# The end of a middle layer and the sums of the next similarity, written as one program for each engine

## The reference, cut to what matters

```
x: 64 batches of 128 x 512 (f32)
layer 0:  A = top-k graph of the mean similarity of x's columns;  x = layernorm(x + An-mixing(x) * adj + bias)
layer 1:  per batch: K = mix of two row-normalised 128x128 kernels of x;  x = layernorm(x + K x W_V' W_O')
layer 2:  as layer 0, on the x that layer 1 gives (a new similarity, a new graph)
layer 3:  x = layernorm(x + (adj*adj)' x + bias)
similarity: x_norm = x / norm over the batches;  S = sum over batches and rows of x_norm x_norm'  (512 x 512)
```

## Time and profile before

| | us |
|---|---|
| median of 3 runs (lowest to highest) | 1667.31 (1666.35 to 1667.31) |
| the profiled execution, own time | 1667.62 |
| its span in the trace | 1665.8 |
| busy in the span: PE | 1513.1 (91%) |
| DVE | 1224.0 (73%) |
| ACT | 926.9 (56%) |
| POOL | 549.3 (33%) |

### The profile page before, as it was taken

How to read it: one execution, slowest core, us unless ns; L and a number is a source line. 1 busy time by engine, 2 the same in 40 slices (tenths; PEclk the granted TensorE clock), 3 DMA queues, 4 the chain that set the end, 5 groups by cost and what they waited for, 6 DMA issues and landing times. The chain is left out here.

```text
span 1665.8 us, 27716 instructions
## 1 busy us (share of the span) xinstructions
PE 1513.1 (91%) x7736; PEld 1255.1 (75%) x7736; DVE 1224.0 (73%) x3081; ACT 926.9 (56%) x1651; POOL 549.3 (33%) x749
## 2 busy tenths in 40 slices
PE   6899999589999999999999999993999971999996
PEld 4677787478888888888888888872888871777774
DVE  5788799647666667666667666653676997799997
ACT  7775455225556554556554556553333870577775
POOL 6553001011223322223322223321000000899997
PEclk9999999689999999999999999996999895999998
DMA  6220393311121221121221121101541000344442
GB/s 216 102 89 1 144 404 147 99 54 44 51 70 63 76 76 42 51 72 63 76 76 40 51 73 63 39 27 63 196 141 38 0 0 6 128 145 145 139 149 103
DMA packets 80630, 148.23 MB, mean 89 GB/s; under 512 B 8448, under 2 KB 8576, under 8 KB 80576
## 3 DMA queue, kind: packets, MB, share of 16 engines
q1 hardware_dynamic: 80576, 147.56, 25.5%
HBM read 97.06 MB, written 50.46 MB: 89 GB/s over the span
## 5 line engine op out<-in xcount | busy, mean ns | idle before, releaser
L814 POOL TENSOR_TENSOR rs_a<-ve_a,neghalf 128x1 f32<-128x1 f32 x64 | 35.1, 548 | 408.8 <-DVE nm_a L808 408.8
L226 PE MATMUL bank<-xn_lo,xn_hi 128*128 128x512 f32 (+1 forms) x640 | 145.4, 358 | 5.4 <-DVE xn_lo L203 5.2
L198 ACT ACTIVATE xn_hi<-xn 128x512 fp32r<-128x512 f32 x128 | 80.6, 630 | 116.7 <-DVE xn L191 116.5
L1176 ACT ACTIVATE xo<-xo,nb_b,rs_b 128x512 f32<-128x512 f32 x64 | 52.2, 816 | 144.9 <-POOL nb_b L816 144.9
L1692 POOL TENSOR_TENSOR xw_lo<-xres,xw_hi 128x512 fp32r<-128x512 f32 x64 | 83.0, 1297 | 131.4 <-ACT xw_hi L1657 131.4
L226 PEld LDWEIGHTS bank<-xn_lo,xn_hi 128*128 128x128 f32 x640 | 102.8, 193 | 19.5 <-DVE xn_lo L203 10.4
L1631 PE MATMUL l_ps<-an_hi,xw_hi 128*128 128x512 f32 x256 | 105.2, 411 | 10.1 <-POOL xw_lo L1692 8.7
L960 PE MATMUL l_ps<-an_hi,xw_hi 128*128 128x512 f32 x256 | 103.5, 404 | 11.8 <-DVE xw_lo L1327 11.5
L217 PEld LDWEIGHTS bank<-xn_hi 128*128 128x128 f32 x512 | 95.2, 191 | 24.1 <-ACT xn_hi L198 7.5
L536 DVE MATCH_REPLACE8 work<-best,work 128x520 f32<-128x520 f32 x160 | 108.2, 684 | 0.0
L322 POOL TENSOR_TENSOR sq_lo<-sq,sq_hi 128x512 fp32r<-128x512 f32 x64 | 87.3, 1380 | 61.3 <-ACT sq_hi L289 61.1
(11 more groups left out here) (238 smaller groups left out, 4743.9 us busy)
## 6 DMA issues: line engine op xcount, KB each, us to landing
xr<-in_x SPq DMA_DIRECT2D x32, 512.0 KB, 3.4
xw_dram<-stage SPq DMA_DIRECT2D x64, 256.0 KB, 6.0
stage<-xw_dram SPq DMA_DIRECT2D x64, 256.0 KB, 2.8
stage<-in_x SPq DMA_DIRECT2D x64, 256.0 KB, 2.7
between<-xo SPq DMA_DIRECT2D x64, 256.0 KB, 2.0
xres<-between SPq DMA_DIRECT2D x32, 512.0 KB, 3.7
xin<-between SPq DMA_DIRECT2D x64, 256.0 KB, 2.7
out<-xo SPq DMA_DIRECT2D x64, 256.0 KB, 2.0
```

Source lines behind the costliest of these rows:

```text
L198: self.nc.scalar.activation(self.hi[:, i % 4, :], self.xn[:, i % 4, :], ACT.Copy).then_inc(self.hi_ready, 1)
L226: mm = self.nc.tensor.matmul(out, h[:, c * P:(c + 1) * P], l[:, a:b], start=(i == 0 and c != 1), stop=False, skip_group_check=True)
L814: nc.gpsimd.tensor_tensor(root, var_eps, neghalf, ALU.pow).then_inc(root_ok, 1)
L1176: nc.scalar.activation(xo[:, i, :], xo[:, i, :], ACT.Identity, scale=rs_b[:, i:i + 1], bias=nb_b[:, i:i + 1]).then_inc(xo_ok, 1)
```

## The change

The function `second_similarity` is gone; its work is done inside `gnn_layer_pair`, without a barrier before it. To make room, the big tiles get fixed places on one ground of 80 slots of 512 values: `xres` takes slots 0 to 63, and the weights and tiles of layers 0 and 1 lie in the same slots. Each pair of batches is brought back once the tile under it has been used for the last time. The PSUM banks are shared too: the sums use banks 0 to 6, which are tiles of the middle layers before.

The turn (14, 15, none) is called `nearly`. In it the norms of the first 56 batches are brought in, rooted, capped, inverted and split, and batch 0 is spread, normalised and given its high part. The turn (15, none, none) is called `last`. In it each engine walks through the 64 batches of the sums, and the table `TAIL` says behind which batch each piece of the last group's chain C stands. The norms of the last 8 batches come when the last group's sums of squares are stored, and are prepared in batches 38 to 51. In `last`, `l1` and the last `squares` use bank 7 alone, so that `l1(i)` waits for `residual_b(i-1)`.

No barrier is left ahead of the sums; the one between the sums and the second `adjacency` stays. Elsewhere only the places of tiles and the numbers of PSUM banks differ, and `diagonals` writes its products into `a_l` and `a_g` and not into a tile of its own. Six semaphores that were cleared at the end of the middle layers are now cleared at the end of the kernel.

The core of the diff:

```diff
+AN, U, WOV, AFTER_WEIGHTS = 0, 8, 18, 26
+AFTER_RING = AFTER_WEIGHTS + RING
+STAGE, PARTS, NORMED, SLOTS = 64, 72, 76, 80
+TAIL = {"scaled": 0, "k_sum": 1, "k_turned": 1, "kt": 3, "l1": [3, 7, 11, 15], "residual": [5, 9, 13, 17],
+        "stats": [6, 10, 14, 18], "norm": [8, 12, 16, 20], "square": [9, 13, 17, 21], "squares": 25, "sums_out": 27,
+        "root": 38, "cap": 39, "invert": [40, 43, 46, 49], "rows_hi": 50, "rows_lo": 51}
...
@@ SyncE, behind the loop of full turns @@
+            turn(groups - 3, None, groups - 1)
+            sp.wait_ge(l0_made, 2 + nb)
+            for p in range(4):
+                bring_back(p)
+            sp.wait_ge(filled[0], 1)
+            sp.wait_ge(n2_stored, 16 * (1 + groups - 2))
+            norms(0)
+            for i in range(GRP):
+                sp.wait_ge(xo_ok, GRP * (groups - 2) + i + 1)
+                store(GRP * (groups - 2) + i, i)
+            sp.wait_ge(y_made, 2 * CH * groups)
+            for p in range(4, 8):
+                bring_back(p)
+            store_sums(groups - 2)
+            for p in range(8, nb // 2):
+                sp.wait_ge(sums.normed, 2 * (p - 8) + 2)
...
+                if p in (13, 15, 17, 19):
+                    i = (p - 13) // 2
+                    sp.wait_ge(xo_ok, GRP * (groups - 1) + i + 1)
+                    store(nb - GRP + i, i)
+                if p == 22:
+                    store_sums(groups - 1)
+                if p == 24:
+                    sp.wait_ge(filled[1], 1)
+                    sp.wait_ge(n2_stored, 16 * (1 + groups))
+                    norms(1)
+                if p == known // 2:
+                    for i in range(GRP):
+                        sp.wait_ge(stored[i], 16 * (groups + 1))
+                bring_back(p)
@@ TensorE, in turn @@
+                if last:
+                    spread(1)
+                    for i in range(nb):
+                        if i == 0:
+                            pe.wait_ge(kl_ok, nb)
+                        sums.squares(pe, i)
+                        if i + 2 < nb:
+                            spread(i + 2)
+                        if i == 0:
+                            pe.wait_ge(v_lo_ok, GRP + nb)
+                            pe.wait_ge(n2_out, groups)
+                        sums.crosses(pe, i)
+                        if i == TAIL["k_turned"]:
+                            k_turned()
+                        if i in TAIL["l1"]:
+                            l1(TAIL["l1"].index(i))
+                        if i == TAIL["squares"]:
+                            squares(0)
+                            squares(1)
+                    return
...
                     m_g_turned()
                     a_s_turned()
+                    if nearly:
+                        spread(0)
                     vprod(3)
@@ ScalarE, in turn @@
+                def n_root(k):
+                    act.wait_ge(n2_in[k], 32)
+                    nc.scalar.activation(nrm[k][:], nrm[k][:], ACT.Sqrt).then_inc(n_rooted[k], 1)
...
                 if B:
                     y_hi(1)
+                if nearly:
+                    n_root(0)
+                    nc.scalar.activation(warm[:], s.inv_s2[:], ACT.Exp)
...
                     y_hi(3)
+                if nearly:
+                    rows_hi(0)
                 if C:
                     for i in range(GRP):
                         square(i)
...
                     exp_g()
+                if nearly:
+                    sums.high_part(act, 0)
@@ VectorE, in turn @@
+                if last:
+                    for i in range(nb):
+                        if i:
+                            dve.wait_ge(x_back[i // 2 % 8], 16 * (i // 16 + 1))
+                            sums.normalise(dve, i, xres[:, i, :])
+                            sums.low_part(dve, i - 1)
+                        if i == 0:
+                            coefficients()
+                        if i == TAIL["k_sum"]:
+                            kernel_sum()
+                        if i == TAIL["kt"]:
+                            kt_lo()
+                        if i in TAIL["residual"]:
+                            residual_b(TAIL["residual"].index(i))
+                        if i in TAIL["stats"]:
+                            stats_b(TAIL["stats"].index(i))
...
...
                     stats_b(0)
                     stats_b(1)
+                if nearly:
+                    n_cap(0)
                 if B:
                     y_lo(2)
+                if nearly:
+                    n_invert(0, 0)
+                    n_invert(0, 1)
...
                     stats_b(2)
                     stats_b(3)
+                if nearly:
+                    n_invert(0, 2)
+                    n_invert(0, 3)
...
                     y_lo(3)
+                if nearly:
+                    rows_lo(0)
...
                     kernel_l()
+                if nearly:
+                    dve.wait_ge(x_back[0], 16)
+                    sums.normalise(dve, 0, xres[:, 0, :])
+                if B:
                     kernel_g()
```

More of the change, by code:

```diff
@@ L65, in scope, with ground, place @@
     return sb, ps, sem
+def ground(nc, s, room):
+    base = -(-nc.sbuf_base // 32) * 32
+    room("ground", [P, SLOTS, N])
+    assert nc.sbuf_base >= base + 4 * SLOTS * N
+    def place(name, slot, shape, dt=F32, ahead=0):
+        return nc.alloc_sbuf_tensor_at(f"{name}_{next(SERIAL)}", [P, *shape], dt, offset=base + 4 * (slot * N + ahead))
+    s.place = place
 def over(ap, n):
@@ L255, in first_similarity @@
         sb, ps, sem = scope(nc, ctx)
-        sq, sq_hi, sq_lo = sb("sq", [P, SQ, N]), sb("sq_hi", [P, SQ, N], F32R), sb("sq_lo", [P, SQ, N], F32R)
-        nrm, inv = sb("nrm", [P, N]), sb("inv", [P, N])
-        rows = [sb(f"rows{k}", [P, N], F32R) for k in range(2)]
+        sq_hi, sq_lo = sb("sq_hi", [P, SQ, N], F32R), sb("sq_lo", [P, SQ, N], F32R)
+        sq = s.place("sq", AFTER_RING, (SQ, N))
+        nrm, inv = s.place("nrm", NORMED, (N,)), s.place("inv", NORMED + 1, (N,))
+        rows = [s.place(f"rows{k}", NORMED + 2 + k, (N,), F32R) for k in range(2)]
         n2 = banks[7]
-        sums = Sums(nc, s, sb, sem, banks[:6], banks[6])
+        sums = Sums(nc, s, sem, banks[:6], banks[6])
         loaded = [sem(f"x_loaded{k}") for k in range(8)]
@@ L394, in _ @@
                         add_squares(j)
[L397 to L465, removed]
@@ L478, in adjacency @@
         sb, _, sem = scope(nc, ctx)
[L479 removed]
+        sim = sb("sim", [P, CH, N]) if weights is None else s.place("sim", AFTER_RING, (CH, N))
+        work = sb("work", [P, CH, 8 + N])
         best = sb("best", [P, CH, 8])
[L481 removed]
+        stage = s.stage
         hl_sb, part = stage[:, 0:CH, :], stage[:, CH, :]
@@ L876, in gnn_layer_pair @@
         passed = sem("passed")
+        x_back = [sem(f"x_back{k}") for k in range(8)]
+        filled, n2_in, n_rooted, n_capped, n_inverted, r_hi_ok, rows_ok = (
+            [sem(f"{n}{k}") for k in range(2)]
+            for n in ("filled", "n2_in", "n_rooted", "n_capped", "n_inverted", "r_hi_ok", "rows_ok"))
         block = ctx.enter_context(nc.Block())
@@ L922, in turn, with bring_back, norms, store_sums @@
                     sp.wait_ge(n2_out, 1 + gp + 1)
-                    sp.dma_start(n2[bass.ds(at, GRP), :], sums[:]).then_inc(n2_stored, 16)
+                    sp.dma_start(n2[bass.ds(at, GRP), :], sums_n2).then_inc(n2_stored, 16)
+            ov = out.rearrange("b l n -> l b n")
+            def bring_back(p):
+                sp.dma_start(xres[:, 2 * p:2 * p + 2, :], ov[:, 2 * p:2 * p + 2, :]).then_inc(x_back[p % 8], 16)
+            def norms(k):
+                lo, hi = ((0, known), (known, nb))[k]
+                for half in (0, HALF):
+                    sp.dma_start(nrm[k][half + lo:half + hi, :], n2[lo:hi, :]).then_inc(n2_in[k], 16)
+            def store_sums(gp):
+                sp.wait_ge(n2_out, 1 + gp + 1)
+                sp.dma_start(n2[GRP * gp:GRP * gp + GRP, :], sums_n2).then_inc(n2_stored, 16)
             turn(None, 0, 0)
@@ L1055, in squares, with spread @@
                         mm.then_inc(n2_made, 1)
+                def spread(i):
+                    pe.wait_ge(rows_ok[0 if i < known else 1], 1)
+                    sums.spread(pe, i, i, rows[0 if i < known else 1][:])
                 A, B, C = ga is not None, g is not None, gp is not None
+                last, nearly = C and not B, B and C and not A
+                if last:
[18 more added lines that the diff above has]
+                    return
                 if A:
@@ L1298, in square_lo @@
                     nc.gpsimd.tensor_tensor(sq_lo[:, i, :], sq[:, i, :], sq_hi[:, i, :].bitcast(F32), ALU.subtract).then_inc(sq_lo_ok, 1)
+                nearly = ga is None and g is not None
+                if nearly:
+                    pool.wait_ge(xa_ok, nb)
+                    nc.gpsimd.memset(nrm[0][:], 1.0).then_inc(filled[0], 1)
                 root_a(0)
```

192 lines of the change are left out of this document (132 added, 60 removed).

## The result

The changed kernel takes 1629.95 us (median of 4 runs, 1627.81 to 1630.66) against 1667.31 us, a ratio of 0.9774 with a 95% interval of 0.9761 to 0.9786. It is faster by 37.4 us; the forecast was 30.9 faster, 1636.4 us, with a range that began at 1630.3, so the measured time lies just outside. The profiled execution took 1630.66 us, its span is 1628.9, so 1.8 us still lie around the span.

The account below looks back on a forecast made before the run. PE was taken to bound the sums. Terms of 114.7 + 5.6 + 1.7 + 1.8 + 2.3 = 126.1 us replace 157.35, a gain of 31.2, less 0.3 is 30.9: 1636.4 us, range 1630.3 to 1642.

Parts of the forecast that it names:

- The new places and banks of the full turns: In the full turns, moved tiles and PSUM banks were put at 0 us, bounds -2 and 2.
- another length of the full turns: Sign of a wrong mechanism: the loop of full turns, costed at nothing, has another length than before.
- the four uncertain terms of the seam: Longer turn (14, 15, none) 1.7 us, start of `last` 1.8, delays beside the batches 2.3, semaphore clearing 0.3.
- The pieces of PE's work: In the sums: 64 batches at 1.80 us, 114.7 us, plus 5.6 us for the chain's PE work and two spreads.
- The start of the batches: At the start of `last`, PE's waits between squares(0) and squares(3) lose 1.8 us, bounds 0 and 6.
- DVE's lumps: In the batches with the last group's chain, added DVE and POOL work delays PE by 2.3 us, bounds 0 and 8.
- the 2.1 us that the prediction named as a sign against it: Sign of a wrong mechanism: PE's batches in the tail of the sums take over 2.1 us.
- The turn (14, 15, none): In `nearly`, preparing the norms ahead of its own work makes PE end 1.7 us later, bounds 0 and 5.
- The cover on ACT: In `nearly`, ACT's idle 4.21 us hides two table loads, root and exp, 3.4 us, with 0.8 us to spare.
- The two rules of the Trainium skill: Shared-port exclusion of VectorE and GpSimd would give 1637.7 us; drain at ACT table switches would give 1637.6 us.
- VectorE did not become the bound: Rival in the sums: DVE becomes the bound, losing 8 to 14 us in place of 2.3, about 1645 us; chance 0.12.
- The rival of a low clock at the seam: PE's clock stays low across the seam, four batches at 1.8 us more, 1643.6 us; chance 0.09.

Follow-up runs that it names:

- e1_pad: The kernel before with one unused tile of 32 bytes a partition ahead of ht: 1657.69 us against 1666.28, ratio 0.9945.
- e8_apart: The changed kernel with ht, y, m, v, kt and neighbours 32 bytes further on, the weights staying: 1636.27 us, ratio 0.9818 to the kernel before.
- e6_order: The changed kernel with the first norms' reciprocals and rows_hi(0), rows_lo(0) later, and the last group's chain one batch later: 1626.22 us.
- e2_banks: The kernel before with the changed kernel's map of PSUM banks in the middle layers: 1667.2 us against 1666.28, ratio 1.0003.
- e5_swap: The kernel before with an unused tile of 32 bytes ahead of all weights, so weights and ht both move: 1667.44 us, ratio 1.0001.
- e3_shift: The changed kernel with its whole ground of 80 slots 32 bytes further on: 1630.04 us.
- e4_chain_first: The changed kernel with the last group's chain run as a piece ahead of the batches of the sums, without a barrier: 1649.86 us.

## Why the prediction was wrong, by its own steps

**The step that failed** is "The new places and banks of the full turns I cost at nothing, bounds -2 and 2, since no view of the trace tells places apart." It is a term of -8.1 us (14 turns of 0.58 us). e1_pad has it alone, 8.6 us; e8_apart takes it away and gives 1636.3, the forecast (6.3 us above the changed kernel by the medians, 7.3 by the ratios to the kernel before). The prediction named another length of the full turns as a sign of a wrong mechanism, and this sign came. The trace did hold a hint that I did not use: within one turn, matmuls of one shape had two paces, 228.9 ns in l0 and 233 in yprod and vprod. The bound of 2 us had nothing under it, and the range of 1630.3 to 1642 left even that out: its lower end has the four uncertain terms of the seam at 0 and the places at 0 too. 14 repetitions of a turn that is bound by PE deserved a bound per matmul: with 108 matmuls of yprod and vprod a turn, 5 ns each are 7.6 us.

**The pieces of PE's work** (64 batches of 1.80, 5.6 us of the chain and the spreads) were right: from 1175.0 on the batches of the changed kernel run at 1.80 us wherever nothing stands between. Only the rounding is off: 64 batches by the sum's own figures, less the two spreads, are 115.0 us and not 114.7.

**The start of the batches** was put at 1.8 us and is 1.9: from squares(0) at 1125.26 to squares(3) at 1132.96 it takes 7.70 us, and three batches and k_turned are 5.8. (The 1.0 us that stands in the expectation of e6_order was counted from the spread of batch 1 to that of batch 4, between which lie only two of three `crosses`.) The order of waits was as told: spread(2) behind normalise(1) behind coefficients, an idle 0.93 us, and shorter ones behind it.

**DVE's lumps** were put at 2.3 us and are 3.0, by the batches over 1.80 us less PE's own additions. The pairs behind residual_b and stats_b take 1.95 and 2.14 us, 0.5 us for each of four, as the sum had it. The reciprocals, of which I wrote that they hardly show, take 0.15 us each, 0.6 in all. The 2.14 us, and 2.17 once, are at the edge of the 2.1 us that the prediction named as a sign against it. Start and lumps together are 4.9 us against 4.1, most of the 0.9 us by which the batches' row of the table falls short.

**The turn (14, 15, none)** was put at 2.0 us longer with its spread and is 2.9, though yprod and vprod got quicker in it. `a_s_turned` waits 1.31 us for ACT in place of 0.37, as the chain over rows_hi and m_out said, and e6_order gives that back. What I had not counted is the clock: behind the same two pauses that left it at 1.00 in the kernel before, it was 0.52 for 3.5 us, in which 8 matmuls ran. At 0.43 us each in place of 0.23 that is 1.6 us. In e8_apart, where it stayed up, the turn is 1.5 us longer than before.

**The cover on ACT** held: the load, the root, the load and the exp took from 1092.31 to 1095.75, and norm_b followed after 0.76 us of idle time. The two rules of the Trainium skill that I weighed gave 1637.7 and 1637.6 us. Of the drain of 1.38 us behind a table load ("ScalarE: Activation LUTs", "What ACT_TABLE_LOAD costs") the changed kernel's trace shows nothing either: the root starts 1.30 us after the load's start. For the shared port ("SBUF — State Buffer", "Who interferes with whom") the trace agrees that the two engines delay each other: the four sq_lo took 1.29 to 1.75 us and the longest low_part 1.14 in place of 0.685. But the 1.8 us worked out from it do not show, for the batches around them take no longer than the others.

**The rivals.** VectorE did not become the bound, and no batch waited for x or for the second norms. The clock stayed at 1.00 through the sums. The rival of a low clock at the seam was right in kind and had the wrong place and size: some us near 1087, and not four batches. No rival of mine made the kernel faster than forecast: all had the seam for their place.

## What to carry to other kernels

A change that moves tiles is a change of every matmul that reads them. Before such a term is put at nothing, compare the pace of matmuls of one shape in the trace; two paces are a reason to ask whether the places matter, and one unused tile tests it. Where a chain of small steps stands alone before a stage bound by one engine, put it between that stage's pieces: here 26 us in the open became 10 us (5 of matmuls and 5 of delay).

## What the runs showed of the hardware

A 512-column fp32r matmul of yprod is 233 ns from start to start where the starts of its two SBUF operands differ by 32 bytes from a multiple of 64 (the kernel before, e2_banks, e5_swap, e8_apart), and 227 ns where the difference is a multiple of 64 (the changed kernel, e1_pad, e3_shift), whichever of the two is off. vprod goes from 233 to between 229 and 230. The matmuls of layer 2 go from 229.8 to 233.2 ns in e3_shift, where their two operands came apart.

It is not a rule for every matmul. `squares` keeps 231 to 233 ns in all of them, and the 256-column matmuls of mprod 118.8 to 119.4. And `l1` goes with yprod (230.4 ns in the kernel before, e2_banks and e5_swap, 228.9 in e8_apart, 226.7 in the changed kernel, e1_pad and e3_shift), although the distance between its own operands is a multiple of 64 in all seven. So what is shown is that the place of these tiles against that of the weights sets the pace. That it acts within a matmul, by its own two operands, is not shown, and why it counts at all no run here shows.

The granted clock can fall behind pauses that leave it up in another execution. Nine profiles have the two pauses of PE before and behind `k_turned`, of 1.35 to 1.38 and 1.50 to 1.51 us, between 1079 and 1095 us of the span. It stayed at 1.00 in the kernel before, e2_banks and e8_apart, and fell in e1_pad, e3_shift, e4_chain_first, e5_swap, e6_order and the changed kernel. The pace of yprod alone does not decide it, for e5_swap has that of the kernel before. In the changed kernel it cost 1.6 us. That it makes part of the spread between runs of one kernel is likely and not shown.
